# First graph layer of a two-layer attention network: f32 products replaced by three f16 products over weights built in place

## What is computed

```python
def _L0_gnn_ref(h, adj, W, a):            # the layer that the change is about
    wh = h @ W
    e = wh @ a[:128, :] + (wh @ a[128:, :]).T
    e = jnp.where(e > 0, e, 0.2 * e)      # leaky relu
    e = jnp.where(adj > 0, e, NEG_BIG)
    return jax.nn.elu(softmax(e, axis=-1) @ wh)

h = jnp.maximum(_layernorm(x, axis=-1), 0.0)
x = x + _L0_gnn_ref(h, adj, L0_gnn_W, L0_gnn_a)
h = jnp.maximum(_layernorm(x, axis=-1), 0.0)
x = x + _L1_gnn_ref(h, adj, L1_gnn_Wq, L1_gnn_Wk)   # cosine attention over the same adj
```

## Time and profile before

| | |
|---|---|
| median of 3 runs | 2465.29 us (2465.23 to 2467.15) |
| span of the profiled execution | 2463.6 us |
| share of the span that an engine is busy | PE 97%, PEld 81%, DVE 87%, ACT 71% |
| prologue, until the first line-982 matmul | 0 to 52 us |
| first layer on PE | 52 to 992 us |
| middle part | 992 to 1077 us |
| second layer | 1077 us to the end |

### The profile page before, as it was taken

One profiled execution on the slowest core, in us unless ns is written; L12 is line 12 of the kernel. 1 busy time (PEld: TensorE's weight loads), 2 busy tenths in 40 slices (PEclk: granted clock), 3 DMA queues, 4 the chain that ended last, 5 costly groups with the idle time before them and its releaser, 6 DMA issues.

```text
span 2463.6 us, 62421 instructions
## 1 busy us (share of the span) xinstructions
PE 2390.4 (97%) x24203; PEld 2006.0 (81%) x24203; DVE 2133.0 (87%) x1653; ACT 1756.8 (71%) x1654; POOL 1.4 (0%) x9
## 2 busy tenths in 40 slices
PE   6999999999999999799999999999999999999999
PEld 5899999999999999667776776776767767767777
DVE  7989898989898988898887888888888878878887
ACT  6567676777777776677776776776777767767776
POOL 0000000000000000000000000000000000000000
PEclk9999999999999999999999999999999999999999
DMA  4798888888888879245565665655655556556563
GB/s 184 256 323 295 304 293 309 304 303 307 299 309 287 318 281 327 68 151 204 203 216 180 210 213 178 217 205 190 213 201 201 202 188 217 192 197 215 205 205 120
DMA packets 153299, 572.05 MB, mean 232 GB/s; under 512 B 9872, under 2 KB 10320, under 8 KB 152784
## 3 DMA queue, kind: packets, MB, share of 16 engines
q1 hardware_dynamic: 143952, 549.26, 63.7%
q10 hardware_dynamic: 9216, 20.98, 2.2%
HBM read 557.58 MB, written 12.62 MB: 231 GB/s over the span
## 4 chain that ended last, share of the span: by engine, by line
PE 91%; DVE 4%; issue 3%; ACT 1%; DMA 0%; SPq 0%; DVEq 0%; ACTq 0%
PE bank L982 35%; PE bank L1067 28%; PE bank L1050 27%; DVE v_sum L742 1%; PE bank L998 1%; DVE hl_buf L620 1%; DVE p_ring L762 0%; DVE hl_buf L802 0%; DVE p_ring L632 0%; PE bank L1009 0%; DVE norm L791 0%; DVE v_buf L809 0%; DVE q_buf L809 0%; PE bank L928 0%; DMA wqk_sb<-wqk 0%
## 5 line engine op out<-in xcount | busy, mean ns | idle before, releaser
L982 PE MATMUL bank<-v_buf,p_ring 128*128 (+1 forms) x8192 | 920.2, 275 | 10.5 <-DVE p_ring L770 6.0
L982 PEld LDWEIGHTS bank<-v_buf,p_ring 128*128 128x128 f32 x8192 | 917.8, 192 | 12.2 <-issue 10.9
L529 ACT ACTIVATE p_ring<-bank 128x1024 f32<-128x1024 f32 x512 | 523.8, 1024 | 386.2 <-PE bank L1050 386.0
L1067 PEld LDWEIGHTS bank<-u_buf,hl_buf 128*128 128x128 f16 x12288 | 721.7, 97 | 61.9 <-issue 2.2
L835 DVE SCALAR_TENSOR_TENSOR p_ring<-adj_ring,p_ring 128x2048 f32<-128x2048 int32 x256 | 586.6, 2292 | 204.4 <-ACT p_ring L529 204.4
L1067 PE MATMUL bank<-u_buf,hl_buf 128*128 (+2 forms) x12288 | 742.7, 220 | 1.2 <-issue 1.1
L1050 PE MATMUL bank<-v_buf,q_buf 128*128 (+1 forms) x3072 | 711.1, 381 | 21.2 <-issue 19.1
L770 DVE SCALAR_TENSOR_TENSOR p_ring<-adj_ring,p_ring 128x2048 f32<-128x2048 int32 x255 | 584.6, 2292 | 75.6 <-DVE p_ring L762 29.9
L840 DVE TENSOR_TENSOR hl_buf<-p_ring,hl_buf 128x2048 f16<-128x2048 f32 x256 | 584.6, 2284 | 0.0
L1050 PEld LDWEIGHTS bank<-v_buf,q_buf 128*128 (+1 forms) x3072 | 291.8, 98 | 329.1 <-issue 29.6
L535 ACT ACTIVATE hl_buf<-p_ring 128x2048 f16<-128x2048 f32 x256 | 487.1, 1903 | 0.6 <-DVE p_ring L835 0.6
(11 more groups left out here) (94 smaller groups left out, 432.6 us busy)
## 6 DMA issues: line engine op xcount, KB each, us to landing
adj_ring<-adj SPq DMA_DIRECT2D x512, 1024.0 KB, 4.9
x_dram<-q_buf ACTq DMA_DIRECT2D x8, 512.0 KB, 5.5
h_dram<-hl_buf ACTq DMA_DIRECT2D x8, 512.0 KB, 5.7
hl_buf<-h_dram SPq DMA_DIRECT2D x16, 256.0 KB, 2.7
r_ring<-x_dram ACTq DMA_DIRECT2D x16, 256.0 KB, 3.7
r_ring<-h_dram ACTq DMA_DIRECT2D x16, 256.0 KB, 3.9
out<-r_ring ACTq DMA_DIRECT2D x16, 256.0 KB, 3.8
r_ring<-a_rows SPq DMA_DIRECT2D x7, 512.0 KB, 5.5
```

The lines of the kernel that those rows point to most:

```text
L529: nc.scalar.activation(p_ring[:, k, hf * 1024:(hf + 1) * 1024], bank[:, 2 * hf:2 * hf + 2, :].rearrange("p b n -> p (b n)"), ACT.Exp, scal ...
L982: ins = mm(acc0(par, it), p0(k)[:, it // 4, jj, f], v_buf[:, bass.ds(j * VW, D + 1)], start=start, stop=False, skip_group_check=True)
L1067: ins = mm(o, hl_buf[:, ps, k, f], v.rearrange("p o c -> p (o c)"), start=head and m == 0 and it % 2 == 0 and (ps, us) == (0, 0), stop=tai ...
```

## The change

The first layer is rewritten. The second is as it was, except that `adj_ring` and `p_ring` are now the two halves of one ring of 8 slots.

- **Words.** Row factor and column factor are made once as 32-bit words that hold an f16 high part (upper 16 bits) and an f16 low part. The larger of two such words, compared as f32, is the word of the larger number. The column's other factor is folded into the values, so that a weight is the maximum of a row word and a column word, times the mask.
- **In place.** A slot holds `adj` as loaded; ACT overwrites it with `sign(adj)` as f32 (0.0 or 1.0); DVE overwrites that with `max(row word, column word) * mask`, in two `scalar_tensor_tensor` of 1024 elements; PE reads the high and the low half of each word as f16 with a step of two elements. A slot is thus held from its load until PE has used it, and SP reloads on `s_used`.
- **Products.** For each stationary place three f16 matmuls in place of one f32 matmul (high by high, high by low, low by high), with values split in high and low f16. In chunks 1 to 7 the pieces of the epilogue stand behind steps 3, 7, 10, 11, 15 and 19 on DVE and 5, 9, 13 and 17 on ACT. The split of the values is made during the first chunk: 16 pieces of 4 blocks, each a product on DVE, a copy to f16 on ACT and a subtraction on DVE.
- **Around it.** `v_sum` now comes from one matmul with the sums of the transposed rows, which ACT accumulates in the prologue. The row words of every chunk, the first included, go out to DRAM and come back by a broadcast; ACT's exponential per chunk is gone. In chunks 1 to 6 SP issues the row load first, with its wait for the end of DVE's work on the chunk before, and then the `adj` loads of that chunk.

```diff
+RING0 = 8
...
-        adj_ring = sb("adj_ring", [P, RING, STEP], I32)
-        p_ring = sb("p_ring", [P, RING, STEP])
+        ring = sb("ring", [P, RING0, STEP])
+        adj_ring = ring[:, 0:RING, :].bitcast(I32)
+        p_ring = ring[:, RING:2 * RING, :]
+        def weights0(k, part):
+            return slot(k, F16).rearrange("p (b j n s) -> p b j n s", b=2, j=2, s=2)[:, :, :, :, 1 - part]
...
-            for k in range(RING):
+            for k in range(RING0):
                 load0(0, k, k)
-            sp.wait_ge(s_atc, 1)
-            sp.dma_start(a_rows[:, :], at_sb[:, :]).then_inc(s_aw, 16)
+            sp.wait_ge(s_word, 2)
+            sp.dma_start(a_rows[:, :], row_word).then_inc(s_aw, 16)
             sp.wait_ge(s_aw, 16)
+            load_r(0, 0)
...
-                        sp.wait_ge(s_p, RING * (G0 * c + g - 1) + k + 1)
-                        load0(c, RING * g + k, k)
+                        sp.wait_ge(s_used, U0 * c + RING0 * (g - 1) + k + 1)
+                        load0(c, RING0 * g + k, k)
+                if not last:
+                    if not first:
+                        sp.wait_ge(s_p, U0 * c)
+                    load_r(c + 1, 1 - par)
                 if not first:
                     group(0)
-                if not last:
-                    if not first:
-                        sp.wait_ge(s_p, RING * G0 * c)
-                    load_r(c + 1, 1 - par)
...
-                        nc.scalar.activation(dst, row, ACT.Relu, bias=ns_col[:, bass.ds(j, 1)],
-                                             scale=f_col[:, bass.ds(j, 1)]).then_inc(s_half, 1)
-                        act.wait_ge(s_half, n + 1)
-                        nc.scalar.activation(dst, dst, ACT.Identity, bias=s_col[:, bass.ds(j, 1)]).then_inc(s_odd, 1)
+                    act.wait_ge(s_adj[k], 16 * (G0 * c + u // RING0 + 1))
+                    act.nop(nofuse=True)
+                    nc.scalar.activation(slot(k), slot(k, I32), ACT.Sign).then_inc(s_sg, 1)
...
+                    parts = dict(zip((5, 9, 13, 17), epilogue(c - 1, 1 - par)))
...
-                        V.tensor_scalar(p0(k)[:, :, 0, :], row, f_col[:, bass.ds(j, 1)], s_col[:, bass.ds(j, 1)],
-                                        ALU.mult, ALU.max).then_inc(s_even, 1)
-                        V.scalar_tensor_tensor(p_ring[:, k, :], adj_ring[:, k, :], 0.0, p_ring[:, k, :],
-                                               ALU.is_gt, ALU.mult).then_inc(s_p, 1)
+                    dve.wait_ge(s_sg, n + 1)
+                    for jj in range(2):
+                        half = words0(k)[:, :, jj, :]
+                        ins = V.scalar_tensor_tensor(half, r_ring[:, par, :].rearrange("p (b n) -> p b n", b=2),
+                                                     th_word[:, 2 * u + jj:2 * u + jj + 1], half, ALU.max, ALU.mult)
+                    ins.then_inc(s_p, 1)
...
+                    parts = dict(zip((3, 7, 10, 11, 15, 19), epilogue(c - 1, 1 - par)))
...
+            def value_scaled(q):
+                V.tensor_tensor(vz_ring[:, q % 2, :, :], v0[:, ZT * q:ZT * q + ZT, 0:D + 1], f4,
+                                ALU.mult).then_inc(s_vz, 1)
+            def value_low(q):
+                dve.wait_ge(s_vh, q + 1)
+                V.tensor_tensor(tiles[:, :, VW:VW + D + 1], vz_ring[:, q % 2, :, :], tiles[:, :, 0:D + 1],
+                                ALU.subtract).then_inc(s_vl, 1)
...
-                                ins = mm(acc0(par, it), p0(k)[:, it // 4, jj, f], v_buf[:, bass.ds(j * VW, D + 1)],
-                                         start=start, stop=False, skip_group_check=True)
+                                for ps, us in parts:
+                                    ins = mm(acc0(par, it), weights0(k, ps)[:, it // 4, jj, f],
+                                             v2[:, bass.ds((2 * j + us) * VW, D + 1)],
+                                             start=start and (ps, us) == (0, 0), stop=False, skip_group_check=True)
```

More of the change, by code:

```diff
@@ L36 @@
 IT0 = C0 // P
[L37 removed]
+U0 = T // (STEP // C0)
+G0 = U0 // RING0
 IT1 = IW // P
[L39 removed]
 G1 = T // (STEP // IW) // RING
@@ L47 @@
 ALPHA = 0.2
-LIFT = 30.0
-EMPTY = 1e-36
+LIFT = 10.0
+LIFT_V = 4.0
+BELOW = 1.0 - 2.0 ** -11
+EMPTY = 2.0 ** -110
 COS_EPS = 1e-4
-VSUMS = 8
+ZT = 4
 UNIT = 64.0
@@ L436, in chunk @@
                 first = isinstance(c, int) and c == 0
[L437 to L446, removed]
[L447 to L458 removed]
                 if first:
[L461 to L467 removed]
+                    parts = {2 * q - 3: (lambda q=q: value_high(q)) for q in range(2, T // ZT)}
+                    value_high(0)
+                    value_high(1)
+                else:
+                    parts = dict(zip((5, 9, 13, 17), epilogue(c - 1, 1 - par)))
+                for u in range(U0):
+                    k = u % RING0
+                    act.wait_ge(s_adj[k], 16 * (G0 * c + u // RING0 + 1))
+                    act.nop(nofuse=True)
+                    nc.scalar.activation(slot(k), slot(k, I32), ACT.Sign).then_inc(s_sg, 1)
+                    if u in parts:
+                        parts[u]()
             def copy_ht(g, r):
@@ L678, in _ @@
[L678 to L681 removed]
+            top_a, top_nb, top_b = (ab_top[:, i:i + 1] for i in range(3))
+            V.tensor_scalar(ab_col[:, 0, :], ab_col[:, 0, :], top_nb, None, ALU.min).then_inc(s_ab, 1)
@@ new lines, in _, with split_words @@
+            dve.wait_ge(s_ab, 11)
+            V.tensor_tensor(f_col[:, :], f_col[:, :], v0[:, :, D + 1], ALU.add).then_inc(s_ab, 1)
+            dve.wait_ge(s_ab, 12)
+            V.scalar_tensor_tensor(shift[:, 3:4], shift[:, 2:3], 0.0, top_b, ALU.max, ALU.add).then_inc(s_ab, 1)
+            dve.wait_ge(s_ab, 15)
+            V.tensor_scalar(shift[:, 4:5], shift[:, 3:4], -1.0, LIFT_V, ALU.mult, ALU.add).then_inc(s_ab, 1)
+            def split_words(word, x, done, first):
+                halves = word.bitcast(F16).rearrange("p (n s) -> p n s", s=2)
+                V.tensor_scalar(halves[:, :, 1], x, BELOW, None, ALU.mult).then_inc(done, 1)
+                dve.wait_ge(done, first)
+                V.tensor_tensor(halves[:, :, 0], x, halves[:, :, 1], ALU.subtract).then_inc(done, 1)
@@ L727, in epilogue @@
                 return denominators, negative, residual, moments, scales, split
-            def first_masks():
-                mask = adj_ring[:, 0, :].rearrange("p (b j n) -> p b j n", b=2, j=2)
-                dve.wait_ge(s_adj[0], 16)
-                for jj, done in enumerate((s_p_first, s_p)):
-                    if jj:
-                        dve.wait_ge(s_odd, 1)
-                    half = p0(0)[:, :, jj, :]
-                    V.scalar_tensor_tensor(half, mask[:, :, jj, :], 0.0, half, ALU.is_gt, ALU.mult).then_inc(done, 1)
@@ new lines, in chunk @@
+                if first:
+                    parts = {2 * q - 4: (lambda q=q: value_scaled(q)) for q in range(2, T // ZT)}
+                    parts |= {2 * q - 3: (lambda q=q: value_low(q)) for q in range(2, T // ZT)}
+                    value_scaled(0)
+                    value_scaled(1)
+                    value_low(0)
+                    value_low(1)
+                else:
+                    parts = dict(zip((3, 7, 10, 11, 15, 19), epilogue(c - 1, 1 - par)))
+                dve.wait_ge(s_rin[par], 8 * c + 16 - 8 * par)
@@ new lines, in chunk @@
+                dve.nop(nofuse=True)
+                for u in range(U0):
+                    k = u % RING0
+                    n = U0 * c + u
+                    dve.wait_ge(s_sg, n + 1)
+                    dve.nop(nofuse=True)
+                    for jj in range(2):
[3 more added lines that the diff above has]
+                    ins.then_inc(s_p, 1)
+                    if u in parts:
+                        parts[u]()
```

192 lines of the change are left out of this document (78 added, 114 removed).

## The result

The changed kernel takes 2316.7 us (2314.9 to 2318.8) against 2466.2 us of the kernel before on the same chip: ratio 0.9393, 95% interval 0.938 to 0.9406. It is 149.5 us faster. I had forecast 2277 with a range of 2245 to 2335: the range holds it, but the gain is 150 us where I had summed 188.

What follows compares the result with a forecast made beforehand. PE bounded the old first layer. First chunk on DVE to 146.7, six periods of 93.3, then PE's tail and last chunk end it at 804.2 against 992.1: gain 187.9, profiled 2275.7, median 2277 us, range 2245 to 2335.

Steps and rivals of the forecast that it cites:

- PE's price: First layer on PE: 57 ns per f16 matmul, 48 a step in 2.73 us, 89.2 us a chunk.
- rival of the strided weights: PE's first-layer weight reads: 4 bytes paid per column, 111.5 ns a matmul, 2919 us; chance 0.08.
- The start: Head of the first layer: first DVE product at 55.7 us, PE from 58.1, 6 later than before.
- DMA at 359 GB/s: First-layer loads at 2.92 us each, a period of 104.4 us, 2348 us in all; chance 0.09.
- A dear sign: ACT's sign at 2.3 us delays masks: period 97 us, about 2300 us in all; chance 0.10.
- The gap: Head of chunks 1 to 6: SP's wait for DVE runs the load pipe dry; PE idles some 4 us.
- PE bound, no gap: First layer: the ring of 8 covers the row load, PE sets the pace, 2248 us; chance 0.10.
- My table: Times in chunks 1 to 6 from T, DVE's end of the chunk before: moments T + 44.8, end T + 93.3.
- gap of about 11 us: Expected sign on DVE's timeline between two chunks, row load at its front, six places, none before the last chunk.
- the period of 93.3 us: Chunks 1 to 6, DVE's end to DVE's end: 93.3 us each, six of them 706.5 us.
- The first landing: First adj load after the gap: issue and landing 0.4 + 4.9 us, behind 1.25 for the row, so T + 6.6.
- DVE's pitch: DVE's two scalar_tensor_tensor a step: 2.3 us back to back, 2.4 after a wait.

Runs made afterwards that it cites:

- the written-out kernel: All eight first-layer chunks written out without the loop over pairs, on top of the changed kernel with SP's order undone: 2257.2 us, ratio 0.9158.

## Why the prediction was right, and where it was off

**PE's price: right.** I took 57 ns for an f16 matmul from the second layer; it is 57.4. The last chunk takes 90.9 us where I had 89.2 + 1.3. The rival of the strided weights (2919) is out: contiguous weights change nothing.

**The start: right.** DVE's first product at 54.92 (55.7 in the sum), PE at 57.55 (58.1). The first chunk is paced by DVE as I said, but DVE ends it at 148.5 where I had 146.7: it takes 93.6 us where I had 91, for which its pitch (below) is enough, and it started 0.8 us earlier. PE ends it at 152.52 + 2.00 = 154.5.

**DMA at 359 GB/s: out.** 382 GB/s in the last chunk, 392 in the written-out kernel, 405 with less PE work. The full stretches of the earlier trace rows were the right reading, not the mean share of the earlier trace rows; they also speak against the figure of some 358 GB/s that the Trainium skill gives in "SBUF — State Buffer", section on bandwidth pools. What a core gets beside a busy neighbour no run here shows.

**A dear sign: out.** 1910 ns, where a copy of that size had 1903.

**The gap: its place and cause right, its size too small.** It stands in six places and not before the last chunk, and goes with SP's order. My table had DVE start again at T + 8.5, and it starts at T + 10.3 to T + 11.0; the "gap of about 11 us" among the signs was counted to the end of the first step, which comes at T + 13.1. *PE bound, no gap* (2248) was the rival for a kernel that did not exist yet: undoing the order and the loop gave 2257.

**The term that was mis-sized is the period of 93.3 us; from DVE's end to DVE's end the six measured 97.7 to 99.4, with a mean of 98.8.** On PE the mean is 99.4, because PE falls further behind DVE on the way. The last mask of chunk 6 is the 24th of the 32 in the first line here (712.28 + 28.79 = 741.07), and PE is done with the chunk at 750.96:

```profile
712.28 38.36 DVE L781 SCALAR_TENSOR_TENSOR ring<-r_ring,th_word,ring 128x1024 f32<-128x1024 f32 x32
...
296.87 56.94 PE L985 MATMUL bank<-v_buf,ring 128*128 x960 [2.01 <-DVE ring L781]
...
296.00:303.00 7.00, 6.13 (x78) 6.10 (x79) 7.00 (x7) 5.70 (x4) 0.00 (x0) 0.76 0.99 384
```

The layer ends 37.8 us later than my 804.2 (842.0). Of these 1.8 come from the first chunk, six times 5.5 = 33 from the periods, and 2.7 from PE, which ends chunk 6 9.9 us behind DVE where I had 7.2; the last chunk adds the rest. PE's 2.7 are the clock in the main: after its 2 us wait for the moments (second line, chunk 2) the granted clock is 0.76 in the 7 us of the third line, and the 20 steps behind take 56.9 us where 20 x 2.755 would be 55.1. Held against my table, in the timeline of chunk 2 (T = 246.26), which is the longest of the six:

| | my table | measured | of the error |
|---|---|---|---|
| first sign starts | T + 6.6 | T + 8.6 | 2.0 |
| moments done | T + 44.8 | T + 48.0 | 1.2 |
| DVE done | T + 93.3 | T + 99.4 | 2.9 |

```profile
294.06 0.17 DVE L604 SCALAR_TENSOR_TENSOR small<-small 128x8 f32<-128x8 f32 x1
...
316.82 28.79 DVE L781 SCALAR_TENSOR_TENSOR ring<-r_ring,th_word,ring 128x1024 f32<-128x1024 f32 x24
```

- *The first landing.* I took 4.9 us from issue to landing from loads that are mostly alone in flight. At the gap seven are issued in a burst behind the row. Even with 32 KB in front, the first took 6.4 us (250.52 to 256.88; 5.4 to 6.9 in the six gaps of that run).
- *DVE's pitch.* I took 2.3 us a step from a `scalar_tensor_tensor` of 1.22 us without a pointer operand. The new ones have one and take 1.28, so 2.4 a step; over the 26 steps that DVE paces this is 2.6 us. The run with a constant confirms the term, though only 1.75 of it shows in the period.
- *ACT at step 18.* The timeline has DVE wait 0.99 us for ACT behind the normalised rows, which I had only for a dear sign. With the 2.0 and the 2.6 above that makes 5.6 of the 6.1; the last 0.5 stays open:

```profile
304.37 3.20 ACT L440 ACTIVATE hl_buf<-q_buf,nbias,rstd 128x128 f32 x8 [2.67 <-DVE nbias L610]
...
308.05 9.12 ACT L464 ACTIVATE ring<-ring 128x2048 f32<-128x2048 int32 x5 [0.48 <-ACT hl_buf L440]
310.06 4.87 DVE L781 SCALAR_TENSOR_TENSOR ring<-r_ring,th_word,ring 128x1024 f32<-128x1024 f32 x4 [0.99 <-ACT ring L464]
```

**Not seen at all: the jump back.** The trace of the kernel before has it, at the same two places on DVE and at no other chunk boundary:

```profile
402.55 0.81 DVE L762 TENSOR_SCALAR p_ring<-r_ring,f_col,s_col 128x1024 f32<-128x1024 f32 x1 [3.00 <-PE bank L982]
...
634.97 0.81 DVE L762 TENSOR_SCALAR p_ring<-r_ring,f_col,s_col 128x1024 f32<-128x1024 f32 x1 [3.13 <-issue]
```

PE was the bound there and did not stop. In the kernel with SP's order undone the pause on DVE is 6.0 and 6.7 us, and PE has one too. The bodies of both engines have grown (DVE's steps are written out, PE's groups hold 8 slots of 48 matmuls for 4 of 16), but no run shows how the pause goes with the size. In the changed kernel the jump adds nothing to the period: chunk 3, behind a jump, has 451.15 - 353.65 = 97.5 us, less than chunk 2 with 100.4. There DVE waits 10 us for loads anyway. It appears once the gap is gone.

**What the change gave, then.** PE's own work in a step fell by 1 - 57.4 x 48 / (111.5 x 32) = 23%, from 3.57 to 2.76 us, which is 208 us in 256 steps. Of these 59.5 were given back: 46.6 by one wait that was moved ahead of eight loads, and 12.9 by the jumps (10.6 of them seen in the layer).

## What to carry to other kernels

When PE's work shrinks until DVE and DMA stand within 10% of it, look for what makes the pipe run dry. Here a wait in the in-order queue cost PE nothing while eight loads stood ahead of it; once it stood ahead of them, it cost the whole refill of the pipe. Price a refill by the landing of a burst, not by the median of single loads, and price a vector instruction by a row with the same kinds of operands. A ring that is held from load to last use needs slots for the whole round trip: here 8 slots gained 192 us over 4.

## What the runs showed of the hardware that I had not expected

- A pointer operand costs a `scalar_tensor_tensor` of 1024 elements 53 ns (1278 against 1225).
- f16 weights read with a step of two elements load as fast as neighbouring ones (97 against 96 ns; 66.28 against 66.17 us for 1152 matmuls).
- A jump back to a large body stopped PE for 4.3 and 2.6 us and DVE for 6.0 and 6.7 (3.0 and 3.1 in the kernel before), and the profile can put the pause down to an engine that had long been done. On PE it cost 6.0 and 4.3 us of the period, since the granted clock was 0.59 and 0.57 behind it.
- DMA keeps 405 GB/s from HBM over 400 us beside busy engines, with a mean share of 1.02; a share of 0.85 at 305 GB/s was no sign of a ceiling near 359.
